# A two-layer step recurrence on one core: 32 moving columns instead of 2 or 4 in most of TensorE's small products

## The chip, the cores and the metric

The kernel runs on one NeuronCore of one Trainium2 chip. The metric is the device time of one execution in microseconds (us). Three runs of the kernel before took 2111.23, 2111.53 and 2111.78 us; their median is 2111.53 us.

## What is computed

The input x is 2 sequences (B = 2) of 1024 steps (T) of 256 features (D). A first layer adds to x a modulated linear map of itself. A second layer adds the output of an LSTM that runs over the 1024 steps:

```
x = x + (x * ys) @ weight * d                  # ys and d are worked out from cond and weight
xW = x @ Wx + b                                # all steps at once, 4*256 columns
for t in range(1024):                          # h = cond, c = 0 at the start
    a = xW[t] + h @ Wh                         # [2, 1024]: gates i, f, o, g of 256 each
    i, f, o = sigmoid(a[:, :768]) in three;  g = tanh(a[:, 768:])
    c = f * c + i * g
    h = o * tanh(c)
out = x + all the h
```

The loop over t is serial: each step's products need the h of the step before. The gate weights Wh are 256 x 1024, the h of a step is 256 x 2.

## The kernel before, in words

**Layout.** Features lie on the 128 partitions, so 256 features are K = 2 chunks. A gate has two output chunks of 128, and each is the sum over two chunks k of h. An h column is one sequence of one chunk, so a chunk of h has B = 2 columns.

**Ahead of the loop.** TensorE transposes x (128 columns, 32-bit floats), projects it (512 columns) and computes xW (512 columns) into SBUF. This ends some 90 us into the span.

**One step.** To keep the precision, Wh is held as two 16-bit halves (`wh_p[:, 0]` and `wh_p[:, 1]`), and so is h (`h_parts[:, 0]` and `h_parts[:, 1]`). The xW of a step comes as three bf16 parts out of a ring that GpSimd fills (`split`, L228 to L240). On TensorE a step of the loop is, in program order (`iteration`, under `@block.tensor`):

1. wait for `c_done` of the step before, then 12 matmuls against an identity that put xW of the gates into PSUM (`input_apart`, `input_together`; 2, 4 or 8 moving columns);
2. wait for `h_hi`, then 8 products for gate I with h's high half (2 columns each);
3. wait for `h_lo`, then 8 products for gate F with both halves of h side by side (4 columns), which signal `f_mm`;
4. 8 for gate G (4 columns, `g_mm`), 8 for gate I with the low half (2 columns, `ig_in`), 4 for the first chunk of gate O (4 columns, `o0_mm`), 4 and 4 for its second chunk (2 columns, `o_mm`).

That is 44 products and as many weight loads of 128 x 128, each product with weights of its own. All matmuls are issued by one helper, so they have the line L302 in the profile; they are told apart by their inputs (`ring,ident_b` or `h_parts,wh_p`).

**The other engines of a step.** VectorE sums F's columns over the two parts of h (L608), then G's (L610), multiplies (L612), sums the first chunk of O (L614), computes the cell by a scan (L617, which signals `c_done`), the high half of h (L620, `h_hi`) and the low half (L623, `h_lo`), and keeps h (L627). ScalarE does the sigmoid of F (L692), of I and G together (L695), of O's two chunks (L697, L699), and the tanh of the cell (L701). The order is written out by hand on each engine, and semaphores carry the step's number.

**PSUM.** Gates I, F, O and G and O's second chunk have a bank of 512 columns each. The results of a gate's chunks stand side by side at its start; the rest of the bank is not read in the loop, except for 128 columns of the bank of G's sum, where 28 transposes of finished output go (L464).

Of the kernel before, what the change touches and what calls it, by code (L numbers as in the profile page):

```python
# [23 lines left out]
ALU = mybir.AluOpType  # L24
ACT = mybir.ActivationFunctionType
AX = mybir.AxisListType

P = 128
# [2 lines left out]
HALF = UNROLL // 2  # L31
EPS = 1e-8
TILE_STEP = 2
H_SCALE = 12
W_TOP = 14
EXPONENT = 0x7F800000
GATE_I, GATE_F, GATE_O, GATE_G = range(4)


I_BANK, G_SUM, F_BANK, O_BANK, G_BANK, FO_SUM, CELL, O_REST = range(8)  # L40
BANK_OF_GATE = (I_BANK, F_BANK, O_BANK, G_BANK)


def cond_resid_lstm(nc, x, cond, w, wx, wh, bias, out):
    B, T, D = x.shape
    K = D // P
    M = wx.shape[1] // P
    G = M // K
    CB = K * B
# [6 lines left out]
    with ExitStack() as ctx:  # L56
# [35 lines left out]
        wh_p = sb("wh_p", [P, 2, K, G * D], F16)  # L92
# [9 lines left out]
        scan_in = sb("scan_in", [P, 6 * CB + 2 + 2])  # L102
        scan_a = scan_in[:, 0:3 * CB].rearrange("p (c s) -> p c s", s=3)
        scan_b = scan_in[:, 3 * CB + 2:6 * CB + 2].rearrange("p (c s) -> p c s", s=3)
        sig_ig = scan_in[:, 2:6 * CB + 2].rearrange("p (h c s) -> p h c s", h=2, s=3)[:, :, :, 0]


        scan_h = sb("scan_h", [P, CB, 3])
        h_parts = sb("h_parts", [P, 2, CB, 3], F16)
# [3 lines left out]
        psum = ctx.enter_context(nc.psum_tensor("psum", [P, 8, BANK], F32))  # L113
        banks = [psum[:, i, :] for i in range(8)]

        pre_f = banks[FO_SUM][:, 0:CB]
        pre_o = banks[FO_SUM][:, CB:CB + B]
        pre_g = banks[G_SUM][:, 0:CB]
        pre_ig = psum[:, I_BANK:G_SUM + 1, 0:CB]
        turned = banks[G_SUM][:, BANK - P:BANK]  # L120
        cell = banks[CELL][:, 0:3 * CB].rearrange("p (c s) -> p c s", s=3)

# [22 lines left out]
        ig_in = sem("ig_in")  # L145
        f_act, o0_act, o_act = sem("f_act"), sem("o0_act"), sem("o_act")
# [147 lines left out]
        def _(pe):  # L294
# [6 lines left out]
            def mm(out_, lhs, rhs, first, last):  # L301
                return nc.tensor.matmul(out_, lhs, rhs, start=first, stop=last, skip_group_check=True)  # L302
# [7 lines left out]
            bank = start_group(("var",))  # L310
            pe.wait_ge(s_ys2, 1)
            pe.wait_ge(s_w2, 1)
            for m in range(K):
                for k in range(K):
                    last = mm(bank[:, m * B:(m + 1) * B], w2[:, k, m * P:(m + 1) * P], ys2[:, :, k], m == 0 and k == 0, k == K - 1)
# [25 lines left out]
            bank = start_group(("h0wh",))  # L341
# [3 lines left out]
            for m in range(M):  # L345
                for k in range(K):
                    last = mm(bank[:, m * B:(m + 1) * B], wh_sb[:, k, m * P:(m + 1) * P], h0[:, :, k], m == 0 and k == 0, k == K - 1)
            last.then_inc(s_filled, 1)

            bank = start_group(("wmax",))  # L350
# [4 lines left out]
            bank = start_group(("scales",))  # L355
# [11 lines left out]
            for n in range(NB):  # L367
                for s, v in last_read("x1", n):
                    pe.wait_ge(s, v)
                for b in range(B):  # L370
                    for m in range(M):
                        bank = start_group(("xw", b, m, n))
                        for k in range(K):
                            last = mm(bank[:, :], wx_sb[:, k, m * P:(m + 1) * P], xt[:, k, b, n * BANK:(n + 1) * BANK], k == 0, k == K - 1)
# [8 lines left out]

            def apart(gate, first, last):

                return banks[BANK_OF_GATE[gate]][:, 2 * B * first:2 * B * last].rearrange("p (c q b) -> p c q b", q=2, b=B)

            def together(bank, first, last):

                return banks[bank][:, B * first:B * last].rearrange("p (c b) -> p c b", b=B)  # L390

            def in_ring(gate, u, part, first, last):
                return ring[:, u, gate, part, B * first:B * last].rearrange("p (c b) -> p c b", b=B)
# [8 lines left out]
            def input_together(gate, bank, u, first, last):  # L402
                for part in range(3):
                    mm_ = mm(together(bank, first, last), ident_b[:, :], in_ring(gate, u, part, first, last), part == 0, True)
                return mm_

            def products(gate, bank, h_part, first, last):

                for c in range(first, last):
                    m = gate * K + c  # L410
                    for k in range(K):
                        for w_part in range(2):
                            mm_ = mm(together(bank, c, c + 1)[:, 0, :], wh_p[:, w_part, k, m * P:(m + 1) * P],
                                     h_parts[:, h_part, k * B:(k + 1) * B, 2], False, True)
                return mm_

            def products_apart(gate, first, last):

                for c in range(first, last):
                    m = gate * K + c  # L420
                    for k in range(K):
                        for w_part in range(2):
                            mm_ = mm(apart(gate, c, c + 1)[:, 0, :, :], wh_p[:, w_part, k, m * P:(m + 1) * P],
                                     h_parts[:, :, k * B:(k + 1) * B, 2], False, True)
                return mm_

            for gate_mm in (f_mm, g_mm, o0_mm, o_mm):
# [47 lines left out]
            for b in range(B):  # L475
                for k in range(K):
                    last = nc.tensor.transpose(banks[B * b + k][:, 0:P], xt[:, k, b, T - P:T], ident[:, :])  # L477
# [3 lines left out]
        def _(dve):  # L481
# [29 lines left out]
            bank = group(("var",))  # L511
# [20 lines left out]
            bank = group(("h0wh",))  # L532
# [9 lines left out]
            bank = group(("wmax",))  # L542
# [45 lines left out]

            def parts_of(gate, chunks):

                return banks[BANK_OF_GATE[gate]][:, 0:2 * B * chunks].rearrange("p (c q b) -> p c b q", b=B, q=2)

            def by_chunk(ap):
                return ap.rearrange("p (c b) -> p c b", b=B)
# [7 lines left out]
            with dve.Fori(0, T // UNROLL) as i:  # L602
                t = i * UNROLL
                for u in range(UNROLL):
                    step = dve.snap(t + u + 2)
                    both = dve.snap((t + u + 1) * 2)
                    dve.wait_ge(f_mm, step)
                    nc.vector.tensor_reduce(by_chunk(pre_f), parts_of(GATE_F, K), AX.X, ALU.add).then_inc(f_sum, 1)  # L608
                    dve.wait_ge(g_mm, step)
                    nc.vector.tensor_reduce(by_chunk(pre_g), parts_of(GATE_G, K), AX.X, ALU.add).then_inc(ig_in, 1)  # L610
                    dve.wait_ge(f_act, step)
                    nc.vector.tensor_tensor(scan_b[:, :, 2], sig_f[:, :], cell[:, :, 2], ALU.mult).then_inc(cell_in, 1)  # L612
                    dve.wait_ge(o0_mm, step)
                    nc.vector.tensor_reduce(by_chunk(pre_o), parts_of(GATE_O, 1), AX.X, ALU.add).then_inc(o0_sum, 1)  # L614

                    dve.wait_ge(cell_in, both)
                    nc.vector.tensor_tensor_scan(flat(cell), flat(scan_a), flat(scan_b),  # L617
                                                 0.0, ALU.mult, ALU.add).then_inc(c_done, 1)
                    dve.wait_ge(t_done, step)
                    nc.vector.scalar_tensor_tensor(out=h_parts[:, 0, :, 2], in0=scan_h[:, :, 1], scalar=2.0 ** H_SCALE,  # L620
                                                   in1=scan_h[:, :, 2], op0=ALU.mult, op1=ALU.mult).then_inc(h_hi, 1)
                    dve.wait_ge(h_hi, step)
                    nc.vector.tensor_tensor_scan(flat(h_parts[:, 1, :, :]), flat(scan_h[:, :, :]), flat(h_parts[:, 0, :, :]),  # L623
                                                 0.0, ALU.mult, ALU.subtract).then_inc(h_lo, 1)
                    if u % HALF == 0:
                        dve.wait_ge(hring_saved, 2 * i + u // HALF + 1)
                    nc.vector.tensor_tensor(hring[:, u, :], scan_h[:, :, 1], scan_h[:, :, 2], ALU.mult).then_inc(h_all, 1)  # L627
# [8 lines left out]
        def _(act):  # L636
# [47 lines left out]
            def iteration(i, n=None):  # L684

                t = i * UNROLL
                for u in range(UNROLL):
                    part = u - TILE_STEP
                    step = act.snap(t + u + 2)
                    both = act.snap((t + u + 1) * 2)  # L690
                    act.wait_ge(f_sum, step)
                    nc.scalar.activation(sig_f[:, :], pre_f, ACT.Sigmoid, scale=unscale).then_inc(f_act, 1)  # L692

                    act.wait_ge(ig_in, both)
                    nc.scalar.activation(sig_ig, pre_ig, ACT.Sigmoid, scale=unscale).then_inc(cell_in, 1)  # L695
                    act.wait_ge(o0_sum, step)
                    nc.scalar.activation(scan_h[:, 0:B, 1], pre_o, ACT.Sigmoid, scale=unscale).then_inc(o0_act, 1)  # L697
                    act.wait_ge(o_mm, step)
                    nc.scalar.activation(scan_h[:, B:CB, 1], banks[O_REST][:, B:CB], ACT.Sigmoid, scale=unscale).then_inc(o_act, 1)  # L699
                    act.wait_ge(c_done, step)  # L700
                    nc.scalar.activation(scan_h[:, :, 2], cell[:, :, 2], ACT.Tanh).then_inc(t_done, 1)  # L701
                    if n is not None and 0 <= part < B * K:
                        b, k = divmod(part, K)
                        if part == 0:
                            act.wait_ge(s_out, n * 16)
                        act.wait_ge(y_turned, n * (B * K) + (part + 2 - B * K))
                        nc.scalar.copy(y_rows[:, b, k * P:(k + 1) * P], turned).then_inc(y_read, 1)
# [39 lines left out]
```

## Time and profile before

| what | value |
|---|---|
| runs | 2111.23, 2111.53, 2111.78 us; median 2111.53 us |
| span of the profiled execution | 2109.4 us |
| median of the runs less that span | 2.1 us |
| TensorE busy (matmuls) | 1884.8 us, 89% |
| TensorE busy (weight loads) | 1744.9 us, 83% |
| VectorE busy | 1250.0 us, 59% |
| ScalarE busy | 707.7 us, 34% |
| GpSimd busy | 480.7 us, 23% |

The span runs from the first to the last instruction of one profiled execution. That execution's own time outside the profile is not given; its span lies 2.1 us below the median of the runs. "Busy" counts the time in which at least one instruction of the engine was under way; matmuls overlap each other, so 89% doesn't mean that the array streams data 89% of the time. The granted clock is a share of 2.4 GHz: 1.00 is 2.4 GHz, 0.50 is 1.2 GHz.

### The profile page before, as it was taken

Reading aid. Unit: us, or ns where it says so; the run is one execution under the profiler, and the core shown is the slowest. Engines: PE = TensorE matmul, PEld = TensorE weight load, DVE = VectorE, ACT = ScalarE, POOL = GpSimd, SP = SyncE. Lnnn points to the kernel's source line nnn. Section 1 sums busy time; section 2 is a strip of 40 time slices with the busy share of each in tenths; the row PEclk is TensorE's granted clock in tenths of the full one; section 3 lists DMA queues with packets and bytes.
Section 4 is the critical chain, followed back from the end, with each engine's and each line's share of the span. In section 5 each row is a group of like instructions: output and inputs, shape, how many; then the busy total and the mean of one; then the engine's idle time right before and its main releaser. Section 6 shows DMA issues by size and latency. Waiting matters only on the chain. (4 is left out here: it accounts for less than half of the span.)

```text
span 2109.4 us, 138886 instructions
## 1 busy us (share of the span) xinstructions
PE 1884.8 (89%) x57612; PEld 1744.9 (83%) x57612; DVE 1250.0 (59%) x8257; ACT 707.7 (34%) x5179; POOL 480.7 (23%) x1298
## 2 busy tenths in 40 slices
PE   8999999999989998899989999899998999989998
PEld 5588888888878888888878888788887888878887
DVE  3366666666656665566656666566665666656665
ACT  2233333333333333333333333333333333333333
POOL 1122222222222222222222222222222222222221
PEclk9855555555555555555555555555555555555555
DMA  2000000000000000000000000000000000000000
GB/s 85 2 0 0 0 0 7 0 0 0 0 8 0 0 0 1 7 0 0 0 1 7 0 0 0 7 1 0 0 0 8 0 0 0 0 8 0 0 0 5
DMA packets 5214, 7.67 MB, mean 4 GB/s; under 512 B 268, under 2 KB 4632, under 8 KB 5144
## 3 DMA queue, kind: packets, MB, share of 16 engines
q1 hardware_dynamic: 4872, 6.30, 0.9%
q8 instruction: 66, 1.08, 0.2%
q10 hardware_dynamic: 272, 0.26, 0.0%
q14 instruction: 4, 0.03, 0.0%
HBM read 4.46 MB, written 2.10 MB: 3 GB/s over the span
## 5 line engine op out<-in xcount | busy, mean ns | idle before, releaser
L302 PE MATMUL psum<-h_parts,wh_p 128*128 128x2 f16 (+1 forms) x45056 | 1370.9, 166 | 12.6 <-issue 12.4
L302 PEld LDWEIGHTS psum<-h_parts,wh_p 128*128 128x128 f16 x45056 | 1286.7, 104 | 28.9 <-issue 12.8
L302 PE MATMUL psum<-ring,ident_b 128*128 128x4 bf16 (+2 forms) x12288 | 492.6, 168 | 202.1 <-DVE psum L617 179.2
L302 PEld LDWEIGHTS psum<-ring,ident_b 128*128 128x128 bf16 x12288 | 409.7, 105 | 286.2 <-DVE psum L617 260.3
L692 ACT ACTIVATE sig_f<-psum 128x4 f32<-128x4 f32 x1024 | 178.0, 174 | 1136.3 <-DVE psum L608 1136.3
L234 POOL CAST ring<-xw 128x64 bf16 (+1 forms) x256 | 121.3, 474 | 1447.2 <-POOLq L272 1413.2
L608 DVE TENSOR_REDUCE psum<-psum 128x4 f32<-128x8 f32 x1024 | 179.2, 175 | 430.9 <-PE psum L302 430.9
L620 DVE SCALAR_TENSOR_TENSOR h_parts<-scan_h 128x4 f16<-128x4 f32 x1024 | 176.5, 172 | 248.4 <-ACT scan_h L701 248.4
L697 ACT ACTIVATE scan_h<-psum 128x2 f32<-128x2 f32 x1024 | 178.2, 174 | 134.3
L610 DVE TENSOR_REDUCE psum<-psum 128x4 f32<-128x8 f32 x1024 | 179.1, 175 | 52.4 <-PE psum L302 13.5
L623 DVE TENSOR_TENSOR_SCAN h_parts<-scan_h,h_parts 128x12 f16<-128x12 f32 x1024 | 187.5, 183 | 35.1
L695 ACT ACTIVATE scan_in<-psum 128x8 f32<-128x8 f32 x1024 | 185.9, 182 | 56.9 <-PE psum L302 13.7
L617 DVE TENSOR_TENSOR_SCAN psum<-scan_in 128x12 f32<-128x12 f32 x1024 | 198.6, 194 | 0.1
L612 DVE TENSOR_TENSOR scan_in<-sig_f,psum 128x4 f32<-128x4 f32 x1024 | 166.0, 162 | 27.2
L701 ACT ACTIVATE scan_h<-psum 128x4 f32<-128x4 f32 x1024 | 181.0, 177 | 0.1
L614 DVE TENSOR_REDUCE psum<-psum 128x2 f32<-128x4 f32 x1024 | 175.1, 171 | 0.5
L699 ACT ACTIVATE scan_h<-psum 128x2 f32<-128x2 f32 x1024 | 172.0, 168 | 0.0
L627 DVE TENSOR_TENSOR hring<-scan_h 128x4 f32<-128x4 f32 x1024 | 154.6, 151 | 0.0
L240 POOL TENSOR_TENSOR ring<-rest,ring 128x64 bf16<-128x64 f32 x256 | 125.2, 489 | 47.6 <-POOLq L228 47.6
L238 POOL CAST ring<-rest 128x64 bf16<-128x64 f32 x256 | 120.7, 471 | 42.9 <-POOLq L228 42.9
L236 POOL TENSOR_TENSOR rest<-xw,ring 128x64 f32<-128x64 bf16 (+1 forms) x256 | 89.4, 349 | 46.3 <-POOLq L228 46.3
L245 POOL TENSOR_TENSOR xt<-xt,hring 128x16 f32 (+1 forms) x256 | 58.3, 228 | 14.8 <-DVE hring L627 14.8
(81 smaller groups left out, 221.8 us busy)
## 6 DMA issues: line engine op xcount, KB each, us to landing
x_rows<-in_x_dram SPq DMA_DIRECT2D x4, 512.0 KB, 8.6
out_dram<-y_rows SPq DMA_DIRECT2D x7, 256.0 KB, 2.1
wh_sb<-in_L_cond_Wh_dram SPq DMA_DIRECT2D x1, 1024.0 KB, 6.0
wx_sb<-in_L_cond_Wx_dram SPq DMA_DIRECT2D x1, 1024.0 KB, 10.9
w_sb<-in_L_cond_weight_dram ACTq DMA_DIRECT2D x1, 256.0 KB, 2.8
out_dram<-y_rows SPq DMA_DIRECT2D x2, 128.0 KB, 1.7
small_rows<-in_cond_dram SPq DMA_DIRECT2D x1, 2.0 KB
small_rows<-in_L_cond_b_dram SPq DMA_DIRECT2D x1, 4.0 KB
```

The costliest lines, as they stand in the source:

```text
L302: return nc.tensor.matmul(out_, lhs, rhs, start=first, stop=last, skip_group_check=True)
L608: nc.vector.tensor_reduce(by_chunk(pre_f), parts_of(GATE_F, K), AX.X, ALU.add).then_inc(f_sum, 1)
L610: nc.vector.tensor_reduce(by_chunk(pre_g), parts_of(GATE_G, K), AX.X, ALU.add).then_inc(ig_in, 1)
L614: nc.vector.tensor_reduce(by_chunk(pre_o), parts_of(GATE_O, 1), AX.X, ALU.add).then_inc(o0_sum, 1)
L617: nc.vector.tensor_tensor_scan(flat(cell), flat(scan_a), flat(scan_b), 0.0, ALU.mult, ALU.add).then_inc(c_done, 1)
L620: nc.vector.scalar_tensor_tensor(out=h_parts[:, 0, :, 2], in0=scan_h[:, :, 1], scalar=2.0 ** H_SCALE, in1=scan_h[:, :, 2], op0=ALU.mult, o ...
L623: nc.vector.tensor_tensor_scan(flat(h_parts[:, 1, :, :]), flat(scan_h[:, :, :]), flat(h_parts[:, 0, :, :]), 0.0, ALU.mult, ALU.subtract).t ...
L692: nc.scalar.activation(sig_f[:, :], pre_f, ACT.Sigmoid, scale=unscale).then_inc(f_act, 1)
L695: nc.scalar.activation(sig_ig, pre_ig, ACT.Sigmoid, scale=unscale).then_inc(cell_in, 1)
L697: nc.scalar.activation(scan_h[:, 0:B, 1], pre_o, ACT.Sigmoid, scale=unscale).then_inc(o0_act, 1)
L699: nc.scalar.activation(scan_h[:, B:CB, 1], banks[O_REST][:, B:CB], ACT.Sigmoid, scale=unscale).then_inc(o_act, 1)
L701: nc.scalar.activation(scan_h[:, :, 2], cell[:, :, 2], ACT.Tanh).then_inc(t_done, 1)
```

## The change

A chunk's columns in the PSUM bank of a gate are now 32 apart (`WIDE = 32`), where they were packed. Every product writes its chunk's 32 columns instead of 2 or 4: the moving operand is the same 2 or 4 columns of h, read again and again by a stride of zero (`broadcast_to`) until there are 32. Only the first 2 or 4 of them are read afterwards. In each call of `products` or `products_apart` the last product is left at its 2 or 4 columns. The calls of a step are seven, so of the 44 products 37 are wide and 7 are as before. The 12 matmuls against the identity keep their columns, at the new places.

```
+WIDE = 32
...
+        def wide(bank, first, last):
+            return banks[bank][:, WIDE * first:WIDE * last].rearrange("p (c n) -> p c n", n=WIDE)
...
+            def spread(bank, c, moving):
+
+                copies = WIDE // (moving.shape[1] * (moving.shape[2] if len(moving.shape) > 2 else 1))
+                columns = wide(bank, c, c + 1)[:, 0, :]
+                if len(moving.shape) > 2:
+                    return columns.rearrange("p (r q b) -> p r q b", r=copies, b=B), moving.unsqueeze(1).broadcast_to([P, copies, 2, B])
+                return columns.rearrange("p (r b) -> p r b", b=B), moving.unsqueeze(1).broadcast_to([P, copies, B])
...
             def products(gate, bank, h_part, first, last):
                 for c in range(first, last):
                     m = gate * K + c
                     for k in range(K):
+                        moving = h_parts[:, h_part, k * B:(k + 1) * B, 2]
+                        columns, copies = spread(bank, c, moving)
                         for w_part in range(2):
-                            mm_ = mm(together(bank, c, c + 1)[:, 0, :], wh_p[:, w_part, k, m * P:(m + 1) * P],
-                                     h_parts[:, h_part, k * B:(k + 1) * B, 2], False, True)
+                            if (c, k, w_part) == (last - 1, K - 1, 1):
+                                columns, copies = together(bank, c, c + 1)[:, 0, :], moving
+                            mm_ = mm(columns, wh_p[:, w_part, k, m * P:(m + 1) * P], copies, False, True)
```

`products_apart` is changed in the same way, with `moving = h_parts[:, :, k * B:(k + 1) * B, 2]` (2 halves of h by 2 sequences). The readers follow the new places: the sums of F, G and O read chunks 32 columns apart (`parts_of`), G's sum is written 32 apart beside I's (`pre_g`), and L695 and its output pattern get one more dimension (`pre_ig`, `sig_ig`); O's second chunk is read at column 32 (L699). They handle as many elements as before.

## Rows read from the trace of the kernel before

**Rows 1.** The page: busy time (us, share, count) and the granted clock in 40 slices.

```profile
PE 1884.8 (89%) x57612; PEld 1744.9 (83%) x57612; DVE 1250.0 (59%) x8257; ACT 707.7 (34%) x5179; POOL 480.7 (23%) x1298
...
PEclk9855555555555555555555555555555555555555
```

**Rows 2.** Busy time by stretch: stretch, length, busy and count per engine, clock, DMA.

```profile
86.00:88.00 2.00, 2.00 (x6) 0.91 (x5) 0.55 (x1) 0.51 (x1) 0.00 (x0) 1.00 0.00 0
...
90.00:92.00 2.00, 1.13 (x45) 1.14 (x46) 0.32 (x4) 0.03 (x1) 0.00 (x0) 1.00 0.00 0
92.00:94.00 2.00, 1.80 (x65) 1.69 (x63) 1.27 (x9) 0.76 (x6) 0.00 (x0) 0.69 0.00 0
94.00:96.00 2.00, 1.82 (x65) 1.72 (x62) 1.24 (x9) 0.71 (x6) 0.00 (x0) 0.50 0.03 8
```

**Rows 3.** Instructions in time order, a steady step: start us, length us, engine, line, idle.

```profile
102.31 0.48 PE L302 MATMUL psum<-ring,ident_b 128*128 128x8 bf16 x12 [0.18 <-DVE psum L617]
102.49 0.17 DVE L620 SCALAR_TENSOR_TENSOR h_parts<-scan_h 128x4 f16<-128x4 f32 x1 [0.24 <-ACT scan_h L701]
...
102.72 1.34 PE L302 MATMUL psum<-h_parts,wh_p 128*128 128x2 f16 x44
...
103.35 0.17 DVE L608 TENSOR_REDUCE psum<-psum 128x4 f32<-128x8 f32 x1 [0.41 <-PE psum L302]
...
103.57 0.17 DVE L610 TENSOR_REDUCE psum<-psum 128x4 f32<-128x8 f32 x1
...
103.78 0.18 ACT L695 ACTIVATE scan_in<-psum 128x8 f32<-128x8 f32 x1
...
103.99 0.19 DVE L617 TENSOR_TENSOR_SCAN psum<-scan_in 128x12 f32<-128x12 f32 x1
...
104.24 0.48 PE L302 MATMUL psum<-ring,ident_b 128*128 128x8 bf16 x12 [0.18 <-DVE psum L617]
```

**Rows 4.** The same view, the loop's first step.

```profile
90.87 0.45 PE L302 MATMUL psum<-ring,ident_b 128*128 128x8 bf16 x12 [1.74 <-DVE psum L586]
...
91.18 1.25 PE L302 MATMUL psum<-h_parts,wh_p 128*128 128x2 f16 x44
91.76 0.17 DVE L608 TENSOR_REDUCE psum<-psum 128x4 f32<-128x8 f32 x1 [1.57 <-PE psum L302]
91.96 0.17 DVE L610 TENSOR_REDUCE psum<-psum 128x4 f32<-128x8 f32 x1
...
92.17 0.18 ACT L695 ACTIVATE scan_in<-psum 128x8 f32<-128x8 f32 x1
...
92.38 0.19 DVE L617 TENSOR_TENSOR_SCAN psum<-scan_in 128x12 f32<-128x12 f32 x1
...
92.63 0.47 PE L302 MATMUL psum<-ring,ident_b 128*128 128x8 bf16 x12 [0.20 <-DVE psum L617]
```

**Rows 5.** The same view, TensorE alone: only the first two matmuls of a run.

```profile
102.31 0.21 PE L302 MATMUL psum<-ring,ident_b 128*128 128x8 bf16 x2 [0.18 <-DVE psum L617]
...
92.63 0.20 PE L302 MATMUL psum<-ring,ident_b 128*128 128x8 bf16 x2 [0.20 <-DVE psum L617]
```

**Rows 6.** Matmuls by shape over the whole span: busy us, mean ns of one.

```profile
L302 PE MATMUL psum<-h_parts,wh_p 128*128 128x4 f16 x20480 | 838.1, 167 | 12.4 <-issue 12.4
```

**Rows 7.** Instructions in time order, TensorE ahead of the loop.

```profile
8.05 6.99 PE L302 MATMUL psum<-small,wh_sb 128*128 128x2 f32 x32 [0.74 <-DVE wh_sb L503]
...
15.06 2.75 PE L325 MATMUL psum<-ident,x_rows 128*128 128x128 f32 x12
...
18.49 1.97 PE L325 MATMUL psum<-ident,x_rows 128*128 128x128 f32 x16
```

**Rows 8.** Matmuls by shape in three stretches: from 8, 15 and 18.8 us.

```profile
L302 PE MATMUL psum<-small,wh_sb 128*128 128x2 f32 x32 | 7.0, 354 | 0.7 <-DVE wh_sb L503 0.7
...
L325 PE MATMUL psum<-ident,x_rows 128*128 128x128 f32 x11 | 2.6, 421 | 0.0
...
L325 PE MATMUL psum<-ident,x_rows 128*128 128x128 f32 x15 | 1.9, 276 | 0.0
```

**Rows 9.** Who waited for whom on TensorE: us in total, times, longest us.

```profile
PE psum L302 <- issue: 33.6, 12, 3.7
```

More of the change, by code:

```diff
@@ L104, in cond_resid_lstm @@
         scan_b = scan_in[:, 3 * CB + 2:6 * CB + 2].rearrange("p (c s) -> p c s", s=3)
-        sig_ig = scan_in[:, 2:6 * CB + 2].rearrange("p (h c s) -> p h c s", h=2, s=3)[:, :, :, 0]
+        sig_ig = scan_in[:, 2:6 * CB + 2].rearrange("p (h c b s) -> p h c b s", h=2, b=B, s=3)[:, :, :, :, 0]
         scan_h = sb("scan_h", [P, CB, 3])
@@ L114, in cond_resid_lstm @@
         banks = [psum[:, i, :] for i in range(8)]
+        def wide(bank, first, last):
+            return banks[bank][:, WIDE * first:WIDE * last].rearrange("p (c n) -> p c n", n=WIDE)
         pre_f = banks[FO_SUM][:, 0:CB]
         pre_o = banks[FO_SUM][:, CB:CB + B]
-        pre_g = banks[G_SUM][:, 0:CB]
-        pre_ig = psum[:, I_BANK:G_SUM + 1, 0:CB]
+        pre_g = wide(G_SUM, 0, K)[:, :, 0:B]
+        pre_ig = psum[:, I_BANK:G_SUM + 1, 0:K * WIDE].rearrange("p h (c n) -> p h c n", n=WIDE)[:, :, :, 0:B]
         turned = banks[G_SUM][:, BANK - P:BANK]
@@ L384, in apart @@
             def apart(gate, first, last):
-                return banks[BANK_OF_GATE[gate]][:, 2 * B * first:2 * B * last].rearrange("p (c q b) -> p c q b", q=2, b=B)
+                return wide(BANK_OF_GATE[gate], first, last)[:, :, 0:2 * B].rearrange("p c (q b) -> p c q b", q=2)
             def together(bank, first, last):
-                return banks[bank][:, B * first:B * last].rearrange("p (c b) -> p c b", b=B)
+                return wide(bank, first, last)[:, :, 0:B]
             def in_ring(gate, u, part, first, last):
@@ L421, in products_apart @@
                     for k in range(K):
+                        moving = h_parts[:, :, k * B:(k + 1) * B, 2]
+                        columns, copies = spread(BANK_OF_GATE[gate], c, moving)
                         for w_part in range(2):
-                            mm_ = mm(apart(gate, c, c + 1)[:, 0, :, :], wh_p[:, w_part, k, m * P:(m + 1) * P],
-                                     h_parts[:, :, k * B:(k + 1) * B, 2], False, True)
+                            if (c, k, w_part) == (last - 1, K - 1, 1):
+                                columns, copies = apart(gate, c, c + 1)[:, 0, :, :], moving
+                            mm_ = mm(columns, wh_p[:, w_part, k, m * P:(m + 1) * P], copies, False, True)
                 return mm_
@@ L589, in parts_of @@
             def parts_of(gate, chunks):
-                return banks[BANK_OF_GATE[gate]][:, 0:2 * B * chunks].rearrange("p (c q b) -> p c b q", b=B, q=2)
+                return wide(BANK_OF_GATE[gate], 0, chunks)[:, :, 0:2 * B].rearrange("p c (q b) -> p c b q", q=2)
             def by_chunk(ap):
@@ L609, in _ @@
                     dve.wait_ge(g_mm, step)
-                    nc.vector.tensor_reduce(by_chunk(pre_g), parts_of(GATE_G, K), AX.X, ALU.add).then_inc(ig_in, 1)
+                    nc.vector.tensor_reduce(pre_g, parts_of(GATE_G, K), AX.X, ALU.add).then_inc(ig_in, 1)
                     dve.wait_ge(f_act, step)
@@ L698, in iteration @@
                     act.wait_ge(o_mm, step)
-                    nc.scalar.activation(scan_h[:, B:CB, 1], banks[O_REST][:, B:CB], ACT.Sigmoid, scale=unscale).then_inc(o_act, 1)
+                    nc.scalar.activation(scan_h[:, B:CB, 1], wide(O_REST, 1, K)[:, 0, 0:B], ACT.Sigmoid, scale=unscale).then_inc(o_act, 1)
                     act.wait_ge(c_done, step)
```

## The prediction

> **What bounds the kernel now.** I read the page first for the clock: TensorE is busy for 89% of the span, yet the granted clock stands at 5 tenths in 38 of the 40 slices [rows 1]. The stretches show when it fell: 1.00 while the 512-column matmuls ran and until 92 us, 0.69 between 92 and 94, and 0.50 from then on [rows 2]. By the 0.69 the fall lies at 92.8 us, 1.9 us into the loop. So the loop's matmuls, with 2 to 8 columns, did not keep the clock at 2.4 GHz, however busy the row calls them.
>
> Then the instructions in order of time, for a step's chain. A steady step lasts from 102.31 to 104.24, 1.93 us [rows 3]. TensorE is in the middle of it: the cell is ready, TensorE begins the xW matmuls (102.31), L620 makes h (102.49), the first product starts at 102.72, the sum of F at 103.35 waits for the sixteenth product, and the sum of G (L610), I and G's sigmoid (L695), the cell's scan (L617) and the next step follow. L627 and the last 12 products (gate O) lie beside this chain. 1023 such steps make 1.93 x 1023 = 1974 us, and the rest of the span is the 91 us ahead of the loop, its ending and 33.6 us in which TensorE waited for its own instructions [rows 9].
>
> **What a product costs.** A product's record lasts 0.167 us [rows 6], but they overlap. 44 of them took 1.34 us at half clock [rows 3], so they start (1.34 - 0.17)/43 = 0.0272 us apart. At full clock 44 took 1.25 us [rows 4], 0.0252 us apart. The half-clock mean includes one longer gap after the wait for h: a first pair of matmuls behind a wait took 0.21 us at half clock [rows 5], a gap of 0.04 to 0.05. Without it I take 0.0267, 32 cycles of 1.2 GHz. Products of 2 columns and of 4 are mixed in that run, and the twelve xW matmuls of up to 8 columns took 0.48 us [rows 3], (0.48 - 0.17)/11 = 0.028 with their long first gap. So the columns do not show: the weight load of 128 columns paces the products.
>
> **The change, part by part.**
>
> *32 columns in 37 of 44 products, at half clock.* 32 columns at 1.2 GHz are 0.0267 us, exactly the spacing that the weight loads already set. Does a stream as long as its weight load still hide beside it? The trace has this case. 32 matmuls of 2 columns in 32-bit floats, paced by weight loads, took 6.99 us, (6.99 - 0.35)/31 = 0.214 apart; the transposes behind them stream 128 columns with the same weight load, and 12 took 2.75 us, (2.75 - 0.42)/11 = 0.212 apart [rows 7, 8]. 126 more columns cost nothing. So the wide products cost 0 at half clock. The bounds: below, nothing can be gained at an unchanged clock. Above, no row has 16-bit moving data read with a stride of 6 bytes for longer than the weight load; if such a read ran at half the rate, each wide product would take 0.0533 us. I take 0, since the nearest row (the transposes) says so; the upper end is kept as the slower rival.
>
> *The last product of a call is narrow.* What a reader waits for ends as before; the wide product in front of it has its stream hidden. 0.
>
> *Sums and sigmoids at the new places.* L608, L610, L614, L695, L697 and L699 treat as many elements as before, L695 with one more dimension. No row has the new patterns. L608 and L610 (one pattern) and L695 take 0.17 and 0.18 us for 8 elements [rows 3], so a stage of that kind is set by its start and not by its elements. I take 0 for all, with 0.01 us a step either way for the three on the path, 10 us over the span.
>
> *xW matmuls.* They write the same number of columns; nothing is added, and no DMA and no queue is touched. TensorE's instructions are as many as before, so the 33.6 us of instruction waits [rows 9] stay.
>
> *The clock.* This decides. Ahead of the loop the trace shows one rise: the transposes from 15.06 us start 0.212 apart and those from 18.49 us (1.97 - 0.28)/15 = 0.113 apart [rows 7, 8], so the clock went from 1.2 to 2.4 GHz between them, after 128-column streams, and not during 6.99 us of 2-column matmuls that were just as busy. (The granted clock has no record of its own before that rise; the durations tell it.) So streaming, and not being busy, went before the rise, and short streams went before the fall [rows 2, 4]. The changed step streams 37 x 32 = 1184 columns where it streamed 24 x 2 + 20 x 4 = 128. At half clock that is 0.99 us of a step of 1.93. No row has a stretch between the transposes and the narrow loop, so whether this raises the clock, and whether it holds at 2.4 GHz, where the same columns take only 0.49 us, can't be read off. I take it that it rises and mostly holds, because the half-clock step lies nearer to the transposes (streaming nearly all the time) than to the loop of before.
>
> The Trainium skill, page "TensorE: Matmul & The Clock Gate", section "Part 1: The HAM clock gate", says that the ratio follows how busy the engine has been and that activity releases the throttle. Taken as busy time it would have the clock up already, with nothing left for this change and a time of 2111; the trace contradicts it, with 89% busy at 0.50, and only in the narrower sense of streaming can it hold.
>
> *What full clock is worth.* Compare the loop's first step (full clock nearly throughout, h and its halves ready beforehand) with the steady one. From the first product to L608: 0.58 against 0.63. From L608 to L617: 0.62 against 0.64. From L617 to the next step's start: 0.25 both [rows 3, 4]. The 0.58 lacks the wait for h, which costs about 0.02 at half clock (a first gap of 0.045 instead of 0.0267) and by the pair at full clock (0.20 against 0.21, [rows 5]) about 0.014 at full clock. So that part is 0.594 against 0.63: 0.036 to 0.04 gained. The part to L617 gains 0.015 to 0.02: at half clock L610 starts 0.22 after L608, waiting for gate G, and at full clock 0.20, bound by VectorE itself. From the step's start to its first product (0.41) the time is ScalarE's and VectorE's, and the xW matmuls (12 x 0.0267 = 0.32) end before it: nothing gained. Sum: 0.056 us a step, between 0.05 and 0.07. What is late next is VectorE and ScalarE, whose 1.3 us of the step don't move.
>
> Some steps stay at half clock: those until the first rise, and some behind each instruction wait (33.6 us in 12 pieces, in which nothing streams). I count 8 of 1023, at the price of 0.5 us in all. 1015 x 0.056 = 57 us. The profiled span would be 2109.4 - 57 = 2052.4 us. The median of the runs is 2.1 us above the span of before (2111.5 less 2109.4), so I forecast **2055 us**, 2.7% less. Its own range is 2040 (0.07 a step) to 2068 (0.05, with the new patterns 0.01 dearer).
>
> **Rivals.**
>
> *The clock alternates.* At half clock the step streams 0.99 us, at full clock 0.49 of 1.87; if the first raises the clock and the second lets it fall, it goes up and down. For it: the loop's first step at full clock was followed by the fall [rows 2, 4]. Against it: that step streamed a tenth of the new one's columns. With half the steps at full clock: 2111.5 - 28 = 2083 us.
>
> *The clock doesn't rise* and the change does nothing. For it: the only rise seen followed streams that left no gaps, and the new step has some 0.9 us with none. Time: 2111 us, within the 10 us of the new patterns, more likely within 2.
>
> *The clock rises but the wide reads pace the products at 0.0267.* 32 columns in 0.0267 us is 1.2 columns per ns; if strided 16-bit data came no faster, full clock would bring only the shorter first gap and a shorter pipe: 0.01 a step, 2101 us.
>
> *The wide reads are slower than their weight load* (the other side). Place: h_parts read by TensorE, in pieces of 2 elements 6 bytes apart, at two places 24 bytes apart for the products of both halves. The point from which it decides: a wide product that takes more than 0.0267 us. Until I's last product 32 have to go, 28 of them wide. A tenth more time for each adds 28 x 0.0027 = 0.075 us a step, 77 us: 2188 us. At half rate it is 28 x 0.0267 = 0.75 us and 2870 us. Against it: 4-column products with both halves start no later than 2-column ones, but there the reading has slack that the wide ones lack at half clock.
>
> The Trainium skill, page "SBUF — State Buffer", section "Door 1: The DMA port swizzle", has a rule against this change: SBUF is read in lines of 16 bytes, and each access that crosses to a new line pays a penalty. By it the two places 24 bytes apart, taken in turn eight times, would pay in every repeat, and the time would be this last rival's. No run here shows it yet: before, such reads were 4 columns long.
>
> **Chances.** Clock up and held 0.37; alternating 0.19; up but paced as now 0.05; no rise 0.26; slower reads 0.13. A measurement of this kernel can't tell less than about 0.2% (4 us) from no change. The first three are faster: 0.61. No rise is within 0.2%: 0.26. Slower by over 0.2%: 0.13. The range is 2040 to 2122 us: it takes in the first four cases and the 10 us of the new patterns, leaves out the slower reads and the tail of the first, some 0.17.
>
> **What would show it.** In the profile after: PEclk of 9 or 10 tenths in the loop (right), a mix (alternating), 5 (no rise). 44 products in about 1.27 us with the clock up; 1.34 at half clock if the wide ones are hidden, more if they are not. The step's gain between the first product and L608 (0.04) and between L608 and L617 (0.015 to 0.02), and none elsewhere. L608, L610 and L695 unchanged in length. The prediction is wrong if the clock stays at 0.50, if wide products start over 0.027 us apart, or if the clock is up and the step is not near 1.87 us.

## The result: 1% slower, and the clock did not move

| | before | changed |
|---|---|---|
| median | 2111.66 us | 2132.49 us |
| lowest to highest, 4 runs | 2111.23 to 2112.52 | 2128.92 to 2138.13 |
| span of the profiled execution | 2109.4 us | 2136.3 us |

The ratio is 1.0101, with a 95% interval of 1.0086 to 1.0117. I had forecast 2055 us and a range of 2040 to 2122 us.

First the page of the changed kernel: busy time and granted clock, as in [rows 1].

```profile
PE 1925.3 (90%) x57612; PEld 1783.0 (83%) x57612; DVE 1271.8 (60%) x8257; ACT 706.1 (33%) x5179; POOL 479.2 (22%) x1298
...
PEclk9855555555555555555555555555555555555555
```

The clock row is the same, digit for digit. The matmuls by shape show that the change does what it says: 37 x 1024 = 37888 wide products.

```profile
L306 PE MATMUL psum<-h_parts,wh_p 128*128 128x32 f16 x37888 | 1400.8, 189 | 11.9 <-issue 11.7 <-DVE h_parts L638 0.2
L306 PE MATMUL psum<-h_parts,wh_p 128*128 128x2 f16 x4096 | 630.4, 166 | 0.0
L306 PE MATMUL psum<-h_parts,wh_p 128*128 128x4 f16 x3072 | 510.0, 166 | 0.0
```

Then a steady step in order of time. The lines answer to [rows 3]; L626, L628, L713 and L635 are L608, L610, L695 and L617 of before.

```profile
1085.09 0.48 PE L306 MATMUL psum<-ring,ident_b 128*128 128x8 bf16 x12 [0.16 <-DVE psum L635]
1085.28 0.17 DVE L638 SCALAR_TENSOR_TENSOR h_parts<-scan_h 128x4 f16<-128x4 f32 x1 [0.25 <-ACT scan_h L719]
...
1085.51 1.38 PE L306 MATMUL psum<-h_parts,wh_p 128*128 128x32 f16 x44
...
1086.14 0.17 DVE L626 TENSOR_REDUCE psum<-psum 128x4 f32<-128x8 f32 x1 [0.39 <-PE psum L306]
...
1086.35 0.17 DVE L628 TENSOR_REDUCE psum<-psum 128x4 f32<-128x8 f32 x1
...
1086.59 0.18 ACT L713 ACTIVATE scan_in<-psum 128x8 f32<-128x8 f32 x1
...
1086.80 0.19 DVE L635 TENSOR_TENSOR_SCAN psum<-scan_in 128x12 f32<-128x12 f32 x1
...
1087.05 0.40 PE L306 MATMUL psum<-ring,ident_b 128*128 128x8 bf16 x9 [0.17 <-DVE psum L635]
```

From the first product to F's sum it is 0.63 us and from there to G's sum 0.21, as before. The next link has grown: from G's sum to L713 it is 0.24, where it was 0.21. What follows is as long as before to 0.01 us. 44 products take 1.38 us instead of 1.34. L713 waits for I's products with the low half of h. Over the records of all steps the median of this link is 0.233 against 0.212 us, and the median step 1.960 against 1.934; the 0.005 us that this link doesn't hold are spread over the others, 0.003 at most in each. 0.026 x 1023 = 27 us, which is the difference of the two spans (26.9). The difference of the medians of the runs is 20.8 us; the changed kernel's runs lie 9 us apart, and the profiled one is the longest of them.

So two questions stand: why are some 32-column products not hidden, when most are? And why did the clock not rise?

### The profile page after: what moved, and what is told of

Same layout as the page of the kernel before. It is cut to its first block and busy times, and to the rows that moved or that the text cites. A ratio compares the mean times of both kernels' runs of the same rounds, so it can differ in the third digit from the quotient of the medians.

```text
span 2136.3 us, 138886 instructions
## 1 busy us (share of the span) xinstructions
PE 1925.3 (90%) x57612; PEld 1783.0 (83%) x57612; DVE 1271.8 (60%) x8257; ACT 706.1 (33%) x5179; POOL 479.2 (22%) x1298
## 5 line engine op out<-in xcount | busy, mean ns | idle before, releaser
L306 PE MATMUL psum<-h_parts,wh_p 128*128 128x32 f16 (+2 forms) x45056 | 1409.4, 185 | 11.9 <-issue 11.7
L306 PEld LDWEIGHTS psum<-h_parts,wh_p 128*128 128x128 f16 x45056 | 1324.9, 105 | 30.7 <-issue 12.2
L626 DVE TENSOR_REDUCE psum<-psum 128x4 f32<-128x8 f32 x1024 | 178.8, 175 | 432.8 <-PE psum L306 432.8
L713 ACT ACTIVATE scan_in<-psum 128x8 f32<-128x8 f32 x1024 | 186.4, 182 | 80.2 <-PE psum L306 13.3
L628 DVE TENSOR_REDUCE psum<-psum 128x4 f32<-128x8 f32 x1024 | 178.8, 175 | 52.3 <-PE psum L306 12.9
L635 DVE TENSOR_TENSOR_SCAN psum<-scan_in 128x12 f32<-128x12 f32 x1024 | 196.4, 192 | 0.1
```

The costliest lines, as they stand in the source:

```text
L628: nc.vector.tensor_reduce(pre_g, parts_of(GATE_G, K), AX.X, ALU.add).then_inc(ig_in, 1)
```

## The experiments

Each experiment gives its ratio to the kernel before as run beside it; the medians of those runs lie between 2106.9 and 2111.7 us, so ratios compare better than times do.

### Why some wide products are slow

All 1024 steps have their products in the same order, so the distance from one product's start to the next can be averaged by its place in the step. Gap 2 is the distance from the second product's start to the third's, and so on. Five kernels (three of them the experiments below), means over the 1018 steps of each whose products run without a break for instructions, worked out from the records, sums in ns:

```
gaps of                              before  changed    e1     e2     e4
I, high half, 7 gaps (2 to 8)           187      188   187    210    188
F and G, both halves, 15 (10 to 24)     400      400   401    401    400
I, low half, and one more, 9 (25 to 33) 240      267   240    240    267
```

In the changed kernel the low half's products cost 27 ns more, and the products of both halves, which have as many wide columns, cost nothing. In the buffer the low half starts 24 bytes behind the high one, and h's columns are 6 bytes apart. From the addresses in the program I worked out that chunk 0's two low columns lie on two sides of a multiple of 16 (and of 64) bytes, while both high ones lie within one stretch of 16. A low product that reads chunk 0, its two columns repeated 16 times, then changes sides with every column. That is four of I's eight low products and two of O's four.

**e1**, the low half 32 bytes behind the high one:

```
-        h_parts = sb("h_parts", [P, 2, CB, 3], F16)
+        h_raw = sb("h_parts", [P, 64], F16)
+        h_parts = h_raw[:, 0:0+2*16].rearrange("p (h x) -> p h x", h=2)[:, :, 0:3 * CB].rearrange("p h (c s) -> p h c s", s=3)
```

> The changed kernel with one edit: the low half of h starts 32 bytes behind the high half instead of 24, so that no pair of its columns spans a multiple of 16 bytes. In the changed kernel the pair of chunk 0 lies at bytes 60 and 66 of a 64-byte frame. Theory A (address): the 32-column products with the low half of h alone are slow because their two source columns lie on two sides of a boundary and are read in turn 16 times. Then the gap from G's sum to L713 goes back from 0.233 to 0.212 us, the step from 1.960 to 1.934 and the time from 2132 to 2111 us. Theory B (time of day): these products are slow because VectorE and ScalarE read PSUM while they write it. Then nothing changes: 1.960 a step, 2132 us. Under both the clock stays at 0.50.

Measured: 2112.21 us (11 runs), ratio 1.001 (1.0001 to 1.0019), median step 1.933. The step in order of time:

```profile
1071.29 1.34 PE L307 MATMUL psum<-h_parts,wh_p 128*128 128x32 f16 x44
1071.93 0.17 DVE L627 TENSOR_REDUCE psum<-psum 128x4 f32<-128x8 f32 x1 [0.39 <-PE psum L307]
1072.14 0.17 DVE L629 TENSOR_REDUCE psum<-psum 128x4 f32<-128x8 f32 x1
1072.35 0.18 ACT L714 ACTIVATE scan_in<-psum 128x8 f32<-128x8 f32 x1
```

1.34 us and 0.21 from G's sum to the sigmoid: back to [rows 3], with all 37 products still at 32 columns. Theory A holds, B falls.

**e2**, both halves moved so that the high half has the divided pair (offset 12 elements, halves 40 bytes apart: `h_raw[:, 12:12+2*20]`):

> The changed kernel with both halves of h shifted: now the high half's pair of chunk 0 lies at bytes 60 and 66 of a 64-byte frame and the low half's within 16 bytes. Theory A (address): I's low products are as fast as before (0.0267 us apart), and the eight products of I with the high half become the slow ones, some 11 ns longer for each group of four, so that the stretch from the first product to the sum of F grows from 0.631 to about 0.655 us and the step is again about 1.96, 2135 us. Theory B (PSUM read by others meanwhile): the high products, which run while nobody reads PSUM, stay fast and the low ones stay slow, 2132 us.

Measured: 2130.97 us, ratio 1.0099 (1.0083 to 1.0114). The cost moved with the address: the high products' gaps grew by 22 ns and the low ones' went back (table). The link from the first product to F's sum is now the longer one, and the one to the sigmoid 0.22:

```profile
1081.46 1.37 PE L307 MATMUL psum<-h_parts,wh_p 128*128 128x32 f16 x44
1082.11 0.17 DVE L627 TENSOR_REDUCE psum<-psum 128x4 f32<-128x8 f32 x1 [0.41 <-PE psum L307]
1082.32 0.17 DVE L629 TENSOR_REDUCE psum<-psum 128x4 f32<-128x8 f32 x1
1082.54 0.18 ACT L714 ACTIVATE scan_in<-psum 128x8 f32<-128x8 f32 x1
```

0.65 us to F's sum (median 0.654, expected 0.655). At that time nobody reads PSUM, so B falls here too. The median step is 1.953 (expected: about 1.96).

**e3**, all products narrow, the places kept (in both functions `if (c, k, w_part) == (last - 1, K - 1, 1):` becomes `if True:`):

> The changed kernel with all 44 products at 2 or 4 columns; only the places 32 apart in PSUM and the readers' patterns are left of the change. Theory A and B both: 1.934 us a step and 2111 us, the same as before. A rival, that the readers' new patterns cost the 21 us: 2132 us with products 0.0267 us apart.

Measured: 2111.42 us, ratio 1.0002 (0.9993 to 1.0011). The readers' new patterns cost nothing.

**e4**, the low half 40 bytes behind, so that its chunk 0 pair spans a multiple of 16 only (`h_raw[:, 0:0+2*20]`):

> The changed kernel with the low half of h 40 bytes behind the high half: the pair of chunk 0 lies at bytes 12 and 18 of a 64-byte frame, across a multiple of 16 but of neither 32 nor 64. If the boundary that counts is 16 bytes: slow low products as in the changed kernel, 1.960 us a step. If it is 32 or 64: 1.934 us a step and 2111 us.

Measured: 2134.09 us in 2 runs, ratio 1.0111 (1.009 to 1.0132), median step 1.960, the low products' gaps 267 ns again. The boundary that counts is 16 bytes. The Trainium skill, page "SBUF — State Buffer", section "Door 1: The DMA port swizzle", gives lines of 16 bytes and a penalty for each access that crosses to a new one; e1, e2 and e4 agree with that. They don't agree with how I had applied it: the products of both halves change lines too, three times in four columns for chunk 0 and twice for chunk 1 by the addresses, and stay at 26.7 ns. With 32 columns, only changing with every column shows.

### Why the clock did not rise

e5 to e10 start from e1, whose wide products are hidden. The columns that the expectations count for a step are rough; by the program they are 1252 in e1, 1668 in e5, 2436 in e6, 1844 in e8, 2484 in e9, 1892 in e10 and 816 in e11.

**e5**: three matmuls more per step, in TensorE's waits (the expectation says two, but `filler(352)` makes two by itself). They stream weights into unread columns of F's bank.

```
+            def filler(columns):
+                for at in range(0, columns, 256):
+                    n = min(256, columns - at)
+                    mm(banks[F_BANK][:, P:P + n], wh_p[:, 0, 0, 0:P], wh_p[:, 0, 1, 0:n], True, True)
...
+                    filler(64)
                     pe.wait_ge(h_hi, t + u + 1)
...
                     products(GATE_O, O_REST, 1, 1, K).then_inc(o_mm, 1)
+                    pe.wait_ge(f_sum, t + u + 2)
+                    filler(352)
```

In e5 and e7 the fillers are marked as the start of a sum in F's bank, and these two kernels compute something else for it (off by 5%). I take it that F's gate loses its xW, which no run shows by itself. From e9 on they aren't marked so; the instructions are the same in number and kind.

> The kernel of e1 (wide products at the spacing of before) and two matmuls more per step that stream 16-bit weights into unread columns of F's bank: 352 columns behind the last product, where TensorE waits some 0.34 us for the cell, and 64 columns between the xW matmuls and the first product. They fit into the waits at half clock (0.29 and 0.05 us), so the step should not grow by them. Columns streamed per step 1728 instead of 1312, 1.4 of 1.93 us at half clock. If the clock follows streaming and e1 was short of it: granted clock up in the loop, step 1.87 to 1.88 us, 2055 us. If it doesn't rise: 0.50 and 2112 to 2125 us.

**e6**: `WIDE = 64`. **e7**: both.

> The kernel of e1 with 64 columns in the 37 wide products. At half clock 64 columns take 0.0533 us, twice the weight load, so TensorE streams nearly without a gap from the first product to the last. No rise of the clock: products 0.0533 us apart where wide, 28 of them ahead of I's last: 0.75 us a step more and some 0.2 more for gate O, about 2.9 us a step and 3080 us. Rise: 0.027 to 0.029 us apart, about the step of before, 2110 to 2150 us.

> e6 with the two fillers of e5: TensorE streams columns for most of every step. If any stretch of the loop is to be like the gapless transposes ahead of the loop, behind which the clock rose, it is this. Rise and held: 1.95 us a step, 2110 to 2150 us, clock near 1. Rise and fall in turn: between. No rise: about 2.9 us a step, 3080 us, and something else than the streaming of columns must have raised the clock there.

Measured: e5 2110.83 us, ratio 1.0015 (1.0004 to 1.0027); e6 2241.13 us, ratio 1.063 (1.0599 to 1.0661); e7 2233.81 us, ratio 1.0595 (1.0565 to 1.0626). The clock rows of e5, e6 and e7, in this order:

```profile
PEclk9955556555566555655556555655556655555565
```

```profile
PEclk9999999999989999999989999899998999989999
```

```profile
PEclk9999999999999999999999999999999999999999
```

The mean clocks are 0.611, 0.979 and 0.988, where e1 has 0.522. So more columns in the loop can raise the clock. In e5 it rises and falls all the time, and its gain is about eaten: 0.041 us in the minority of steps that ran at full clock, against instruction waits that grew with the code (six times in the loop a wait falls across two steps, which took some 9.3 us together before and some 9.9 in e5). In e6 the clock holds, but its products start some 30 ns apart, which is more than the 26.7 ns that 64 columns are at 2.4 GHz. From the step in order of time:

```profile
1132.27 1.46 PE L307 MATMUL psum<-h_parts,wh_p 128*128 128x64 f16 x44
1132.94 0.17 DVE L627 TENSOR_REDUCE psum<-psum 128x4 f32<-128x8 f32 x1 [0.43 <-PE psum L307]
1133.19 0.17 DVE L629 TENSOR_REDUCE psum<-psum 128x4 f32<-128x8 f32 x1
```

44 products in 1.46 us: full clock, and still slower than before's 1.34. The median step is 2.040 us. It was 0.1 us off my "about the step of before", and the times of e6 and e7 lie above the 2110 to 2150 us that I expected. By the records, the products of one half start 28 to 32 ns apart and those of both halves mostly 31; why it isn't 26.7 is open.

**e8**: `WIDE = 48`. **e9**: the same with fillers of 512 and 128 columns. **e10**: `WIDE = 32` with the fillers of e9.

```
-WIDE = 32
+WIDE = 48
...
+                    filler(128)
...
+                    filler(512)
```

> The kernel of e1 with 48 columns in the 37 wide products. In e6 64 columns kept the clock at 2.4 GHz in nearly all of the loop (mean 0.979), but at that clock its products started 0.028 to 0.032 us apart and the step took 2.04 us. 48 columns are 0.020 us at full clock and should hide below the 0.025 us that e5 shows for a product at full clock. If the clock holds as in e6: the step of e5's full-clock stretches, 1.89 us, and 2111 - 1010 x 0.041 = 2070 us. If it rises and falls in turn, each half-clock step has products of 48 columns 0.040 us apart and takes 2.35 us: between 2070 and 2500 us, about 2300.

> e8 with fillers of 512 columns behind the last product and 128 ahead of the first, which fit into TensorE's waits at full clock (0.21 and 0.05 us). 2500 columns per step. Clock held, 1.89 us a step, 2070 us. The fillers add instructions, so the six long instruction waits grow by some 0.6 us each, as in e5. If e8 holds too, e8 is the faster by some 4 us; if only this one holds, the fillers are what holds it.

> The kernel of e1 (32 columns) with the fillers of e9: at full clock some 1950 columns a step, against 2500 in e6 (held) and 1730 in e5 (fell each time). At half clock the filler behind the last product takes 0.43 us where 0.34 are free. Held: 2070 us. Falling in turn: 2080 to 2150 us. No rise: 0.1 a step more, 2210 us.

Measured: e8 2540.34 us, ratio 1.2052 (1.2027 to 1.2076), clock 0.539; e9 2084.17 us, ratio 0.9891 (0.9875 to 0.9908), clock 0.987; **e10 2077.59 us, ratio 0.9864 (0.9847 to 0.988)**, clock 0.983. e8 shows the risk: with the clock down in most of the loop, 48 columns take 0.040 us, and a step 2.37 us. I had expected at most 2500 us for it. It also streams more columns a step than e5 and had the lower clock, so their number in a step doesn't decide alone. e9 has e10's median step (1.892 us), but a step at half clock takes 2.52 us there. One of e8's half-clock steps:

```profile
1284.70 1.83 PE L307 MATMUL psum<-h_parts,wh_p 128*128 128x48 f16 x44
1285.51 0.17 DVE L627 TENSOR_REDUCE psum<-psum 128x4 f32<-128x8 f32 x1 [0.57 <-PE psum L307]
```

e10's start of the loop by stretches (columns as in [rows 2]), and a steady step of it:

```profile
92.00:94.00 2.00, 2.00 (x60) 1.77 (x61) 1.21 (x8) 0.72 (x7) 0.00 (x0) 0.62 0.03 8
94.00:96.00 2.00, 2.00 (x63) 1.79 (x62) 1.18 (x8) 0.63 (x6) 0.00 (x0) 0.53 0.00 0
96.00:98.00 2.00, 1.88 (x62) 1.62 (x62) 1.23 (x8) 0.78 (x6) 0.89 (x3) 1.00 0.00 0
...
400.00:500.00 100.00, 99.41 (x3117) 85.52 (x3114) 61.82 (x422) 35.35 (x263) 24.32 (x66) 1.00 0.00 0
```

```profile
1053.92 0.45 PE L307 MATMUL psum<-ring,ident_b 128*128 128x8 bf16 x12
1054.11 0.17 DVE L647 SCALAR_TENSOR_TENSOR h_parts<-scan_h 128x4 f16<-128x4 f32 x1 [0.24 <-ACT scan_h L728]
1054.24 0.22 PE L307 MATMUL psum<-wh_p 128*128 128x128 f16 x1
...
1054.33 1.27 PE L307 MATMUL psum<-h_parts,wh_p 128*128 128x32 f16 x44
...
1054.94 0.17 DVE L635 TENSOR_REDUCE psum<-psum 128x4 f32<-128x8 f32 x1 [0.36 <-PE psum L307]
1055.14 0.17 DVE L637 TENSOR_REDUCE psum<-psum 128x4 f32<-128x8 f32 x1
...
1055.35 0.18 ACT L722 ACTIVATE scan_in<-psum 128x8 f32<-128x8 f32 x1
...
1055.47 0.38 PE L307 MATMUL psum<-wh_p 128*128 128x256 f16 x2
1055.57 0.19 DVE L644 TENSOR_TENSOR_SCAN psum<-scan_in 128x12 f32<-128x12 f32 x1
```

The clock fell in the same stretch as before ([rows 2]) and came back within the two next stretches. A product to F's sum is 0.61, to G's sum 0.20, to the sigmoid 0.21, to the cell 0.22; the median step is 1.892 us. The rows of `wh_p` are the fillers. They hold nothing up at full clock: from the step's start to its first product it is 0.41 us and from the cell to the next step 0.25, as in [rows 3]. Some 1000 steps gain 0.04 us each, and the longer instruction waits and the few half-clock steps (2.03 us) give a part back: 29 us in the medians of the runs (2106.94 us beside it, and 2077.59).

**e11**: e3 with e10's fillers. **e12**: the changed kernel with e10's fillers.

> e3 (all products at 2 or 4 columns) with the fillers of e10 and nothing else: some 770 columns a step instead of 1950. It asks whether the 32 columns of the change do anything for the clock. If they do: clock near 0.5, each half-clock step 0.09 longer as in e10's (2.03 us), 2200 us. If long streams in the waits are enough: clock near 0.98, 1.89 us a step, 2077 us, as e10.

> The changed kernel as it is (low half of h 24 bytes behind the high one) with the fillers of e10. It asks what the address costs at full clock. If alternating reads have a pace of their own that the array's clock doesn't change (some 0.033 us for 32 columns, from e2 and e4), the low products start 0.028 to 0.033 us apart where e10 has 0.025, 8 of them on the path: 0.04 us a step, 1.93 us, 2118 us. If the pace doubles with the clock: 1.89 us, 2077 us.

Measured: e11 2214.45 us, ratio 1.0492 (1.0474 to 1.0509), clock 0.521, median step 2.027 us. The fillers alone do not raise the clock and cost 0.09 a step; the 32-column products alone (e1) do not either. Together they do. Being busy is not what tells them apart. The busy rows of e11 and of e6, and e11's clock:

```profile
PE 2168.8 (98%) x60684; PEld 1908.3 (86%) x60684; DVE 1246.7 (56%) x8257; ACT 706.0 (32%) x5179; POOL 480.9 (22%) x1298
```

```profile
PE 2041.4 (91%) x57612; PEld 1854.2 (83%) x57612; DVE 1279.2 (57%) x8257; ACT 706.5 (32%) x5179; POOL 492.5 (22%) x1298
```

```profile
PEclk9855555555555555555555555555555555555555
```

e11 was busy for 98% of the span and stayed at half clock; e6 was busy for 91% and held full clock.

e12: 2098.23 us, ratio 0.9943 (0.9926 to 0.996), clock 0.983, median step 1.911 us. Its low products are 28, 32, 29 and 25 ns apart where e10's are 25: the alternating read shows at full clock too, at nearly the same 32 ns as at half clock. It costs 0.019 us a step, not the 0.04 expected: only the pair of chunk 0 pays, 27 ns over gaps 25 to 33.

## Why the prediction was wrong

*What bounds the kernel, the product's cost.* Held. The loop is one chain through TensorE, VectorE and ScalarE, and at half clock a product costs its weight load, 0.0267 us.

*32 columns at half clock cost nothing.* Right for the 27 wide products of the high half and of both halves, and wrong for the low half of h: the extra time shows in its ten wide products (seven of gate I, three of gate O), and by the addresses it comes from the six that read chunk 0. The transposes I took as the nearest row read their data side by side, and I kept 0 as the value. The "slower reads" rival had the right place (pieces two elements long, 6 bytes apart), the wrong victims (all wide products, those of both halves above all) and the wrong size: I charged all 28 wide products with a tenth, 77 us; the runs show some 11 to 13 ns for each four low products, 26 ns a step, 21 us in the medians. e1 to e4 settle it. The term was 0 and measured 0.026 us a step.

*The clock rises and mostly holds.* This step failed, and with it the forecast. I chose it because the new half-clock step lay, as I put it, nearer to the transposes than to the old loop. My own number doesn't say that: 0.99 of 1.93 us is half of the step. The rows gave no value for anything between, and 0.37 was a guess in that gap. The runs show where the changed kernel lies: clock 0.522, as before. So the rival "the clock doesn't rise" is what happened, at 2112 us in e1 (ratio 1.001), plus the low products' 21 us. I had weighed two of my cases as exclusive that came together; their sum, 2132 us, lay 10 us above my range.

*What full clock is worth.* I had 0.056 us a step; e10's full-clock steps gain 0.041 to 0.042. From the first product to F's sum it is 0.609 (median), not 0.594. By the records there is one gap of 39 and one of 28 ns around the ninth product, the first that needs the low half of h: I read it as TensorE getting there before VectorE (L623) has it. For it: the gap of 39 is as long as the one behind the wait for the high half, and at half clock it is 33 ns, but 27 in e11, where the products start later behind L623. No run moved the ninth product. The loop's first step, my row for full clock, had h ready and could not show this wait [rows 4]. I had counted L623 nowhere. The rest (0.20 to G's sum, no gain beyond the cell) was as predicted. The bound of 2068 us in this part should have been 2071: 1015 steps at 0.05 less 0.01 us.

*Sums and sigmoids at the new places, xW matmuls.* Cost nothing (e3).

*Alternating, paced as now.* Alternating happened in e5, with more columns than the change has, but not in the changed kernel. Products at full clock and 32 columns are 25 ns apart in e10, so "paced as now" falls for aligned data.

**What stays open.** What exactly the chip looks at before it raises the clock is not settled by these kernels, and I draw no rule from them. Why e8 stayed down with more columns a step than e5 is part of that. I also didn't try to place the ninth product later, behind work that doesn't need the low half. Why the changed kernel's runs (and e4's) spread over 9 us and e2's over less than 2 is not explained.

## What to carry to other kernels

32 columns streamed beside a weight load were free here unless every column lay in other 16 bytes than the one before it: look at the byte addresses of a repeated or strided moving operand, not only at its length. Padding the stream to win the clock can lose more than it wins: 32 columns (e1) brought nothing, 48 alone lost 20%, and 32 with the waits filled won 1.4%, so test it with the filled waits and read the granted clock before reading the time. And take the price of a faster engine from a step that has all its waits, since a step that starts with its inputs ready hides the next one.

## What the runs showed of the hardware

- The granted clock stayed at 0.50 in the loop with TensorE busy for 90% of the span (changed kernel) and for 98% (e11), and held 1.00 in nearly all of it with 91% (e6). The Trainium skill, page "TensorE: Matmul & The Clock Gate", section "Why this matters for your kernels", advises to keep the engine continuously busy for full clock; taken by the busy row, the changed kernel and e11 contradict it.
- Two matmuls of 16-bit data with weights of their own start 25 ns apart at full clock, with 2 to 48 columns (e10, e9), and 28 to 32 at 64 (e6).
- A pair of columns read in turn across a multiple of 16 bytes, 32 columns in all, makes gaps of up to 32 or 33 ns, at half clock (changed, e4) and at full clock (e12) alike.
